# Rotation tables built on GpSimd in a second buffer, and a weight fetch moved behind three small copies, in a six-layer decoder kernel

## The reference

```python
x = attn_layer(shift_tokens(x), Wqkv[i], q_scale[i], k_scale[i], Wo[i]) + x
x = ffn_layer(shift_tokens(x), ln_g[i], ln_b[i], W1[i], b1[i], W2[i], b2[i]) + x

def shift_tokens(t):                    # the upper 128 channels come from the token before
    a, s = jnp.split(t, 2, -1)
    s = jnp.pad(s, ((0, 0), (1, 0), (0, 0)))[:, :-1]
    return jnp.concatenate([a, s], -1)

# in attn_layer, 16 heads of 64 channels, windows of 64 tokens:
q = l2norm(q) * qs
k = l2norm(k) * ksc
q = q * cos * scale + rotate_half(q) * sin * scale
k = k * cos * inv + rotate_half(k) * sin * inv
```

## Time and profile before

| | us |
|---|---|
| median of three runs | 2654.38 |
| the profiled execution | 2655.91 |
| its span in the trace | 2654.1 |
| TensorE busy (matmuls) | 2580.1 |
| VectorE busy | 2279.5 |
| ScalarE busy | 2059.5 |
| GpSimd busy | 1388.8 |

### The profile page before, as it was taken

The page is one execution under the profiler, slowest core; times in us unless marked ns, Lnnn a source line. Parts: engine busy times, 40 slices in busy tenths (PEclk is TensorE's granted clock), DMA queues, the critical chain, the costliest instruction groups (busy, mean ns, idle before and its releaser), DMA issues.

```text
span 2654.1 us, 77750 instructions
## 1 busy us (share of the span) xinstructions
PE 2580.1 (97%) x25160; PEld 2294.4 (86%) x25160; DVE 2279.5 (86%) x7689; ACT 2059.5 (78%) x6056; POOL 1388.8 (52%) x1438
## 2 busy tenths in 40 slices
PE   8889999999999999999999999999999999999996
PEld 7768888888888888888888888888888888888885
DVE  5579989988998888899888989988999998888883
ACT  5458878877887788788778878877887887787774
POOL 5454546455554645455454545545454555556560
PEclk9989999999999999999999999999999999999998
DMA  5212232424222333322234232243323242311100
GB/s 167 80 53 94 72 98 92 159 75 151 92 71 98 125 127 107 118 89 75 94 135 158 71 118 89 75 148 125 113 71 116 84 150 64 102 32 31 42 25 28
DMA packets 149542, 253.25 MB, mean 95 GB/s; under 512 B 21418, under 2 KB 88202, under 8 KB 148106
## 3 DMA queue, kind: packets, MB, share of 16 engines
q1 hardware_dynamic: 148698, 250.90, 29.1%
q10 hardware_dynamic: 688, 0.39, 0.0%
HBM read 137.14 MB, written 80.55 MB: 82 GB/s over the span
## 4 chain that ended last, share of the span: by engine, by line
PE 88%; DVE 3%; issue 2%; DMA 1%; POOL 1%; ACT 1%; SPq 1%; DVEq 0%; ACTq 0%; POOLq 0%
PE ring L1133 29%; PE ring L1183 14%; PE acc L1158 10%; PE score L1224 7%; PE ring L1237 6%; PE acc L1196 6%; PE ring L1147 6%; PE mix L1251 4%; PE mix L1255 2%; PE mix L1253 2%; PE ring L1167 1%; DMA xn<-res 1%; PE ring L1115 1%; PE acc L1203 0%; DVE probs L1609 0%
## 5 line engine op out<-in xcount | busy, mean ns | idle before, releaser
L1133 PE MATMUL ring<-w_qkv,xT 128*128 128x512 f32 x3456 | 883.0, 400 | 5.4 <-DVE with_sin L1516 4.0
L1133 PEld LDWEIGHTS ring<-w_qkv,xT 128*128 128x128 f32 x3456 | 624.0, 189 | 131.8 <-DVE with_sin L1516 5.4
L1418 POOL TENSOR_SCALAR sums_sq<-sums_sq 128x8 f32<-128x8 f32 x384 | 108.5, 283 | 1052.2 <-DVE sums_sq L1511 1043.9
L1354 ACT ACTIVATE probs<-probs,shift 128x128 f32<-128x128 f32 x1536 | 596.6, 392 | 26.5 <-DVE shift L1593 25.8
L1593 DVE CUSTOM_DVE_ANT_0 probs<-score,mask,query_scale 128x128 f32<-128x128 f32 x1536 | 438.7, 347 | 42.4 <-PE score L1224 35.0
L1183 PEld LDWEIGHTS ring<-nT,w_up 128*128 128x128 f32 x3168 | 395.8, 189 | 21.5 <-issue 6.8
L1183 PE MATMUL ring<-nT,w_up 128*128 128x256 f32 x3168 | 409.6, 282 | 4.3 <-issue 3.6
L1299 ACT ACTIVATE with_sin<-ring 128x512 f32<-128x512 f32 x384 | 228.2, 595 | 213.4 <-PE ring L1133 213.4
L1427 POOL TENSOR_TENSOR sums_sq<-sums_sq,half 128x8 f32<-128x8 f32 x192 | 324.4, 1690 | 16.0
L1424 POOL TENSOR_TENSOR query_scale<-sums_sq,half 128x8 f32<-128x8 f32 x192 | 318.0, 1656 | 22.0 <-POOL sums_sq L1418 11.8
L1372 ACT COPY probsT<-ring 128x512 f32<-128x512 f32 x384 | 226.1, 594 | 108.4 <-issue 103.0
(11 more groups left out here) (153 smaller groups left out, 4419.8 us busy)
## 6 DMA issues: line engine op xcount, KB each, us to landing
w_parts_scratch<-staging SPq DMA_DIRECT2D x120, 519.0 KB, 3.1
staging<-in_w_next SPq DMA_DIRECT2D x60, 519.0 KB, 4.9
w_qkv<-w_parts_scratch SPq DMA_DIRECT2D x20, 1536.0 KB, 9.4
v_mid<-v SPq DMA_DIRECT2D x192, 128.0 KB, 2.3
w_up<-w_parts_scratch SPq DMA_DIRECT2D x20, 640.0 KB, 6.9
y_in<-y_scratch SPq DMA_DIRECT2D x48, 256.0 KB, 3.0
res<-y_scratch SPq DMA_DIRECT2D x48, 256.0 KB, 2.8
y_scratch<-res SPq DMA_DIRECT2D x41, 256.0 KB, 3.2
```

Source lines behind the costliest of these rows:

```text
L1133: last = pe.matmul(bank(item)[:], xT[a][:, h, t * P:(t + 1) * P], w_qkv[w][:, h, c, g, :], start=(h == 0 and (a, w) == PASSES[0]), stop=(h ...
L1354: last = act.activation(probs[:, k, cols], probs[:, k, cols], ACT.Exp, bias=shift[:, k, i:i + 1], scale=-1.0, accum_out=sums[:, k, i:i + 1])
```

## The change

The tables get two buffers, one for odd and one for even layers. In the switch slot, the loads of the next layer's tables and scales are issued first on SP, ahead of the loads of `y_in` and `res`, and the tables' load waits only for the last rotation of the layer before the present one. The four multiplications are done on GpSimd at the start of its switch slot, ahead of `("rotate", 1, 0)`; VectorE only waits for `tables_built` where it did them before. (The first layer's tables are still made on VectorE.) `fetch(0)` moves from ahead of the shift's transfers to right behind them. The kernel is built with `dynamic_dma_scratch_size=1024`, a smaller reserved stretch of SBUF.

```diff
+def build_tables(eng, layer, scales_loaded, tables_loaded, tables_built, tables, qk_scales):
+    eng.wait_ge(scales_loaded, layer * 16 + 16)
+    eng.wait_ge(tables_loaded, layer * 16 + 16)
+    for part in range(2):
+        scale = qk_scales[:, part].unsqueeze(1).broadcast_to([P, TILES, 2, HEAD_DIM // 2])
+        for k, sc in ((0, scale), (1, scale[:, :, ::-1, :])):
+            made = tables[layer % 2][:, 2 * part + k].rearrange("p t (a b) -> p t a b", a=2)
+            last = eng.tensor_tensor(made, made, sc, ALU.mult)
+    last.then_inc(tables_built, 1)
...
-        tables = sb("tables", [P, 4, TILES, HEAD_DIM])
+        tables = [sb(f"tables{i}", [P, 4, TILES, HEAD_DIM]) for i in range(2)]
...
-                wait(sp, parts_ready, layer * (BATCH * ROTATIONS))
-                sp.dma_start(tables[:], D["rope"]).then_inc(tables_loaded, 16)
+                wait(sp, parts_ready, (layer - 1) * (BATCH * ROTATIONS))
+                sp.dma_start(tables[layer % 2][:], D["rope"]).then_inc(tables_loaded, 16)
...
+                if s.switch == "projections":
+                    load_tables(s.layer + 1)
+                    load_scales(s.layer + 1)
                 if s.early and not (isinstance(n, int) and n == -1):
                     wait(sp, input_filled, n * HALVES + HALVES)
                     sp.dma_start(y_in[:], as_tiles(D["y"][s.next_batch])).then_inc(y_loaded, 16)
...
-                if s.switch == "projections":
-                    fetch(0, s.layer)
-                    load_scales(s.layer + 1)
...
                     sp.dma_start(xn[0:1, 1, P:DIM], res[P - 1:P, 0, P:DIM]).then_inc(shifted, 16)
+                if s.switch == "projections":
+                    fetch(0, s.layer)
...
-                if s.switch == "projections":
-                    load_tables(s.layer + 1)
...
+                if s.switch == "projections":      # GpSimd, start of the slot
+                    build_tables(pool, s.layer + 1, scales_loaded, tables_loaded, tables_built, tables, qk_scales)
...
-                        return tables[:, k, t, :]...
+                        return tables[(s.late_layer if g else s.early_layer) % 2][:, k, t, :]...
...
                     if s.switch == "projections" and item == ("rotate", 0, 0):
-                        build_tables(s.layer + 1)
+                        dve.wait_ge(tables_built, s.layer + 2)
...
-    nc = bacc.Bacc("TRN2", target_bir_lowering=False, num_devices=1)
+    nc = bacc.Bacc("TRN2", target_bir_lowering=False, num_devices=1, dynamic_dma_scratch_size=1024)
```

More of the change, by code:

```diff
@@ L1473, in _ @@
         def _(dve):
[L1474 to L1484, removed]
             def dense(s, item):
@@ L1507, in table @@
                     def table(k):
-                        return tables[:, k, t, :].rearrange("p (a b) -> p a b", a=2).unsqueeze(1)\
+                        return tables[(s.late_layer if g else s.early_layer) % 2][:, k, t, :].rearrange("p (a b) -> p a b", a=2).unsqueeze(1)\
                             .broadcast_to([P, GROUP_HEADS, 2, HEAD_DIM // 2])
@@ L1625, in slot @@
                     if isinstance(s.n, int) and s.n == -1 and item == ("rotate", 0, 0):
-                        build_tables(0)
+                        build_tables(dve, 0, scales_loaded, tables_loaded, tables_built, tables, qk_scales)
+                        dve.wait_ge(tables_built, 1)
                     if s.switch == "projections" and item == ("rotate", 0, 0):
-                        build_tables(s.layer + 1)
+                        dve.wait_ge(tables_built, s.layer + 2)
                     if s.does(item):
```

## The result

The changed kernel takes 2666.1 us, the median of five runs (2663.61 to 2668.53), against 2654.91 for the one before (2652.9 to 2657.48, five runs): a ratio of 1.0042 with a 95% interval of 1.0031 to 1.0054. It is slower, by 11 us where 8.5 were forecast. That is 0.4%, with an interval that lies wholly above 1. The profiled execution took 2663.61 us (span 2661.8), 7.7 more than that of the kernel before.

What follows compares the result with a forecast made beforehand. TensorE, its matmuls busy for 97% of the span, was taken to bound the kernel. Five switch slots at 2.55 us each, 12.75, less 4.2 removed, gave +8.5 us: 2663 us for the median, range 2653 to 2670 in 8 of 10.

Steps and rivals of the forecast that it cites:

- GpSimd's lateness: Switch slot: building makes GpSimd 2.9 us late; TensorE stalls 1.1 us (0.3 to 3.2) at turn (1, 3), not added.
- the rival with a chance of 0.10: GpSimd 5 us late in switch slots, turn (1, 3) waits 3.2 us, fetch(0) has landed: +9.8 us, 2664; chance 0.10.
- the wait for the transfer in all five slots: Sign: in each switch slot TensorE waits 1.7 to 4 us for the w_qkv transfer, where no such wait existed.
- the end of VectorE's wait for the copies: Sign: VectorE's wait for the shift's transfers (xn<-res) is gone in the five switch slots.
- GpSimd's first rotation: Sign: in the switch slot it comes about 3 us later, behind four multiplications of some 0.45 us.
- the wait at turn (1, 3): Sign: in the switch slot, a wait of about 1 us for GpSimd's product.
- Bound and pace: TensorE bounds the kernel; regular slots stay at 51.57 us and a slot has no spare time to make up lateness.
- The wait for fetch(0): At unit (0, 0) of each switch slot TensorE waits 2.55 us (1.75 to 3.95), the second transfer landing after 10.9.
- The 0.15 us in it for weights loaded again: At unit (0, 0), a drained TensorE array loads weights again after the wait: 0.15 us of the 2.55.
- What was removed, 4.2 us: The five switch slots' whole excess over the regular slot, all credited to the change as gain: 4.2 us.
- The reading of rows 3: Slots 15 and 31: VectorE waits for the shift's transfers, then TensorE for late probabilities; some 2.8 of the 4.2 us.
- Costed at nothing: Early loads on SP in the switch slot: 1.6 us of issue fits a gap, cost 0, at most 1.6 us.

Runs made afterwards that it cites:

- experiment 2: The changed kernel with the tables multiplied on VectorE ahead of rotate (0, 0), as before; fetch(0) stays moved: 2671.16 us, ratio 1.0064.
- experiment 7: The kernel before the change with only fetch(0)'s second transfer moved behind the shift's copies: 2652.0 us, ratio 0.9994.
- experiment 3: The changed kernel with fetch(0) in its old place and GpSimd building the tables behind the norm's root, ahead of rotate (0, 0): 2660.12 us, ratio 1.0022.
- experiment 4: The changed kernel with GpSimd's build behind the norm's root and fetch(0) split, high parts ahead of the shift's copies, low parts behind: 2655.63 us, ratio 1.0006.
- experiment 1: The changed kernel with fetch(0) back ahead of the shift's copies, GpSimd still building at the slot's start: 2664.31 us, ratio 1.0032.

## Why the prediction came out as it did

The sign and the range were right, and the time, 2663 us, was 3 under the measured 2666.1. That it came so near is in good part luck. The forecast gave 12.75 us to TensorE's waits for fetch(0); these are 2.5 us, in two slots. The rest came by GpSimd's lateness, the path of the rival with a chance of 0.10, and by the clock, which had no place at all. Of the signs that were to show it right, the wait for the transfer in all five slots failed, and so did the end of VectorE's wait for the copies (slots 15 and 31 keep it); GpSimd's first rotation was 4.2 and 3.8 us late (slots 7 and 39) and not 3, and the wait at turn (1, 3) 1.6 to 2.7 us and not 1. The steps:

- **Bound and pace.** Right. TensorE's regular slot stayed at 51.58 us, and next to no lateness within a slot was made up (slots 31 and 39 are each over by 0.3 us less than their two waits).
- **The wait for fetch(0).** The term was right for itself and wrong in the sum. The second transfer took 11.0 to 11.4 us where 10.9 were taken, and alone (experiment 2) the wait is 1.7 to 2.9 us a slot against 2.55 forecast. The 0.15 us in it for weights loaded again is shown by no run: in all seven waits for fetch(0), TensorE starts 0.04 us after the landing. In the changed kernel only 1.1 and 1.5 us of the wait are seen, in two slots, because GpSimd's wait comes first, and in the three other slots the slow clock behind it. The prediction said that GpSimd's stall would be contained in the fetch's; in those three slots it was the other way about.
- **GpSimd's lateness.** The step failed in its size. I had 1.1 us at turn (1, 3); it is 1.6 to 2.7. A multiplication took 462 ns where I had 441, so that was right. The loads were what I mis-sized: in the five switch slots the scales landed 4.1 to 4.9 us after their issue, not 3.5. In slot 7 they were also issued 0.6 us later than in the others, since the store ahead of them on SP took 1.24 us to issue instead of 0.39.
- **The clock.** Missing from the prediction. A fall of the granted clock for 3.4 us behind such a wait costs 1.1 to 1.4 us in three slots, 3.7 in all (what they are over, less the wait). It is what the sum lacked: the two kinds of waiting come to 12.6 us together, by chance almost the 12.75 that were forecast for one of them.
- **What was removed, 4.2 us.** The reading of rows 3 failed: the waits for the shift's copies in slots 15 and 31 were put down to fetch(0), and experiment 7 took its second transfer out of the way with both waits still there. What makes most of them is the instruction packet (experiment 7). In the changed kernel, too, VectorE still waits 1.4 and 0.6 us there. About 0.3 us a slot of VectorE's work is what really went. The split fetch together with the early loads, which remove everything else, stop at 1.9 us.
- **Costed at nothing.** The early loads on SP were not free for fetch(0) (experiment 3: its second transfer takes up to 2.9 us longer, and slots 7, 23 and 39, where VectorE had waited at most 0.2 us for the copies, have waits of 0.9 to 1.3). In the change its move behind the copies hides that.

In sum: 15.8 - 4.2 = 11.6 us, made of 10.1 us of waiting for GpSimd, 2.5 for the fetch and 3.7 of slow clock, which is 16.3, less 4.2 and less the 0.5 that slots 31 and 39 made up.

The Trainium skill ("DMA: Bandwidth & Descriptors", section "Anatomy of one DMA — SWDGE (gpsimd) path") gives a fixed 2.0 us and the bytes at 436 GB/s, as a fit for transfers that GpSimd issues; these here are issued by SyncE, which the prediction did not say. An estimate by it has both parts of the fetch land 9.2 us after the first issue; the trace has 11.5 to 11.9. For the low part alone in slot 7 of experiment 4 the estimate is 2.0 + 3.6 = 5.6 us; the trace has 7.2.

What stays open: how the instruction packet delays the copy; that both share a transfer engine was not seen directly. In the eight experiments' traces and the two kernels', each slot 15 and 31 has such a packet 12.1 to 13.0 us into the slot, and a copy that lands 1.3 to 3.3 us later than the 12.8 of an undisturbed slot. (The 3.3 is slot 15 of experiment 1, where fetch(0) landed only at 15.4.) No run moved the packet in these two slots. Nor is it settled what makes the clock fall: gaps of 1.8 us did it in experiment 1, and one of 1.8 in the changed kernel (slot 31) and one of 2.3 in experiment 2 (slot 23) did not.

## What to carry to other kernels

Work moved to an idle engine is only hidden if its data are there when the idle time begins. Look at where the engine's idle stretch lies, and issue the load before it, not at the point where the work is listed. And do not price two edits that delay the same engine as a sum or as free cover for each other: test each alone, because here each alone cost about as much as both. And before a late transfer is put down to the one queued ahead of it, look for the same lateness in places where that one is not in flight.

## What the runs showed of the hardware

- In ten of the 15 switch slots of the changed kernel and of experiments 1 and 2, gaps in TensorE's otherwise full stream were followed by 3.4 us at the lower clock: in eight slots a single gap of 1.8 to 2.9 us, in two a pair (1.6 and 0.8; 1.2 and 2.3). In the other five, with waits of 0.8 to 2.3 us, it stayed up. Where it fell, a wait of 2.0 us cost 3.2 to 3.4.
- VectorE's TENSOR_SCALAR of 128x128 float32 out of SBUF takes 0.28 us alone and 0.49 beside GpSimd's TENSOR_TENSOR of 128x128 (1.60 against 0.88 for four). GpSimd's own duration did not change: 1.70 us for four either way. The Trainium skill says why such pairs do not share bandwidth ("SBUF — State Buffer", section "SBUF: two separate sides"): the two engines have one pair of ports between them, as an exclusive lock that is held for a whole instruction; VectorE takes part in it with instructions in a mode of two ports or with two inputs in SBUF, and no run here shows the mode of this one. The pace of the four, one VectorE instruction to each of GpSimd's, agrees with it. What GpSimd runs matters: beside its power on 128x8, which takes 1.67 us, the same VectorE instruction took 0.28 to 0.29 in all of the 176 cases of the changed kernel's trace in which it lay wholly within one, so there the trace shows no lock held for the whole of GpSimd's instruction.
- Fetching instructions goes through the transfer queues in packets of 16 KB that take about 1 us. Where one starts 0.5 to 1.8 us behind the issue of the last shift copy, outside the switch slots, the copy lands 1.1 to 2.1 us late (36 of 36 cases; none of the 360 without one), and the slot takes 0.4 to 1.9 us longer.
